# Phase 2 of a hybrid layer: transposes and their copy issued one tile ahead of the matmuls that use them

## Chip, cores and metric

The kernel runs on 8 cores of one Trainium2 chip. Every core runs the same program on its own data: a pair of cores shares one batch row of 8192 tokens, each producing half of it, and nothing is exchanged between cores. The metric is the device time of the slowest core in microseconds.

## What is computed

The reference is a layer of four residual steps on x of shape (4, 8192, 1024), cut here to what matters:

```python
# step 1: state-space like mixing (phases 1 and 2)
xn = layernorm(x)
proj = xn @ W_proj.T
delta, Bs, Cs, residual = split(proj, 4)
delta = softplus(delta @ W_delta.T + b_delta)
y = exp(delta * A1) * B1 * sum(xn * Cs) + cumsum(delta * B1) * sum(Cs)
x = x + y + residual * D
# step 2: feed-forward with a low-rank part folded into the weight (phase 2)
x = x + layernorm(x) @ (W + lora).T + b
# step 3: full self-attention of layernorm(x) (phase 3), then step 2 again
x = x + softmax(q @ k.T / 32) @ v
x = x + layernorm(x) @ (W + lora).T + b
```

## The kernel before

The program is written by hand: a small class collects each engine's instructions in the order in which the Python code adds them (`sch.add`), with waits on counting semaphores in front. So the order of the code is the order on every engine. VectorE, ScalarE and GpSimd also wait for their own previous instruction each time. TensorE has only the waits that are named; a wait whose count was already waited for on that engine is dropped.

Phase 1 (to about 1250 us) runs three 1024x1024 projections over 64 tiles of 128 tokens and writes delta and the residual part to DRAM. Phase 2 (about 1340 to 3500 us) is the subject. It loops over the same 64 tiles. Phase 3 computes attention in four passes over the keys, and in the last pass the second feed-forward.

Phase 2 for tile i consists of these parts:

- `p2loads(i)`: SyncE loads x, delta, the residual part and two carry rows.
- `p2A(i)`: step 1. GpSimd makes `g0b` (line 644) and D (661), TensorE a cumulative sum by a triangular matrix (650) and the carry (655), ScalarE the exponential E (664), VectorE G (666), GpSimd F (670) and D (673), VectorE E (675), and GpSimd the new x in F (679). F is p2F in the profile, and so on.
- `p2Bln(i)`: layer norm of F into `xn2b`, by the helper `ln`, whose lines 191 to 212 stand for all norms: a VectorE sum (191), small steps that alternate between ScalarE and VectorE, and the wide ScalarE step into bf16 (212).
- `p2B(i)`: step 2. Eight TensorE transposes (line 186, helper `transposes8`) into the PSUM tile PT1 or PT2, a ScalarE copy to `xn2T` (line 700), 16 matmuls into PB with `W_eff` (line 707), VectorE adds the bias into G (714), GpSimd adds F into H (717).
- `p2C(i)`: layer norm of H into `xn3b`, stored by ScalarE's queue; for the first 32 tiles H is stored too.

The loop body for i is: `p2C(i)`, `p2loads(i+3)`, `p2A(i+3)`, `p2Bln(i+2)`, `p2B(i+1)`. Buffers xn2b, xn2T, PT and H alternate between two, F and G rotate over three, PB is single.

Of the kernel before, what the change touches and what calls it, by code (L numbers as in the profile page):

```python
# [76 lines left out]
def build(phases=3, dbg=False, cut=None):  # L77
# [55 lines left out]
    TM = lambda m: ("t", m)  # L133
    VM = lambda m: ("v", m)
    SM = lambda m: ("s", m)
# [45 lines left out]
    def transposes8(pt, src_bf, waits=()):  # L181
        m = None
        for c in range(8):
            m = sch.add("tensor",
                        lambda e, o=pt[:, c, :], i_=src_bf[:, c * 128:(c + 1) * 128]:
                        e.transpose(o, i_, s_id[:, :]),
                        waits if c == 0 else (), inc=("t", 1) if c == 7 else None)
        return m
# [68 lines left out]
    try:  # L257
# [48 lines left out]
        for mch in range(8):  # L306
            p = mch % 2
# [297 lines left out]
        if phases >= 2:  # L605
# [11 lines left out]
            xn2b = [C2(nc.sbuf_tensor(f"xn2b{p}", [128, 1024], BF16)) for p in range(2)]  # L617
# [9 lines left out]
            mk2 = {}  # L627
# [58 lines left out]
            def p2Bln(i):  # L686
                p = i % 2
                q3 = i % 3
                mxn2 = ln(F_[q3], xn2b[p], st2[p], (GM(mk2[("x1", i)]),
                                                   TM(mk2.get(("tp2", i - 2), 0))))  # L690
                mk2[("xn2", i)] = mxn2

            def p2B(i):
                p = i % 2
                q3 = i % 3
                PTx = PT1 if p == 0 else PT2
                mxn2 = mk2[("xn2", i)]
                mtp2 = transposes8(PTx, xn2b[p], (SM(mxn2), SM(mk2.get(("ev2", i - 2), 0))))
                mk2[("tp2", i)] = mtp2
                mev2 = sch.add("scalar", lambda e, pp=p, pt=PTx: e.copy(  # L700
                    xn2T[pp][:, :, :], pt[:, :, :]),
                               (TM(mtp2),), inc=("s", 1))
                mk2[("ev2", i)] = mev2
                mf1 = None
                for n in range(2):
                    for k in range(8):
                        mf1 = sch.add("tensor", lambda e, nn=n, kk=k, pp=p: e.matmul(  # L707
                            PB[:, nn * 512:(nn + 1) * 512], xn2T[pp][:, kk, :],
                            W_eff[:, kk * 1024 + nn * 512: kk * 1024 + nn * 512 + 512],
                            start=(kk == 0), stop=(kk == 7)),  # L710
                            (SM(mev2), VM(mk2.get(("x2a", i - 1), 0)), VM(m_weff_v))
                            if (n == 0 and k == 0) else (),
                            inc=("t", 1) if (n == 1 and k == 7) else None)
                mx2a = sch.add("vector", lambda e, qq=q3: e.tensor_add(  # L714
                    G_[qq][:, :], PB[:, :], s_bfbc[:, :]), (TM(mf1),), inc=("v", 1))
                mk2[("x2a", i)] = mx2a
                mx2 = sch.add("gpsimd", lambda e, pp=p, qq=q3: e.tensor_add(  # L717
                    H_[pp][:, :], G_[qq][:, :], F_[qq][:, :]),
                    (VM(mx2a), mk2.get(("sx2", i - 2))), inc=("g", 1))
                mk2[("x2", i)] = mx2  # L720

            def p2C(i):
                p = i % 2
                mxn3 = ln(H_[p], xn3b[p], st3[p], (GM(mk2[("x2", i)]),
                                                   mk2.get(("sxn3", i - 2))))
                mk2[("sxn3", i)] = dma("scalar", sc_xn3[i, :, :], xn3b[p][:, :], ch=f"sx3{p}")
                if i < NQ:
                    mk2[("sx2", i)] = dma("scalar", sc_x2[i, :, :], H_[p][:, :],
                                          (GM(mk2[("x2", i)]),), ch=f"sx2{p}")

            def p2loads(i):
                p = i % 2
                mk2[("lx", i)] = dma("sync", A_[p][:, :], x_d[i * 128:(i + 1) * 128, :],
                                     (GM(mk2[("x1", i - 2)]),), ch=f"lA{p}")
                mk2[("lhi", i)] = dma("sync", hilo[p][0:1, :], sc_hi[i:i + 1, :],
                                      (TM(mk2[("tri", i - 2)]),), ch=f"lh{p}")
                mk2[("llo", i)] = dma("sync", hilo[p][1:2, :], sc_lo[i:i + 1, :], ch=f"lh{p}")
                mk2[("ldl", i)] = dma("vector", B_[p][:, :], sc_delta[i, :, :],
                                      (GM(mk2[("eIn", i - 2)]), mk[("dst", i)]), ch=f"lB{p}")
                mk2[("lr", i)] = dma("vector", Cc_[p][:, :], sc_res[i, :, :],  # L740
                                     (VM(mk2[("x1a", i - 2)]), mk[("rst", i)]), ch=f"lC{p}")
# [4 lines left out]
            p2A(2)  # L746
            p2Bln(0)
            p2Bln(1)
            p2B(0)
            for i in range(NT):  # L750
                p2C(i)
                if i + 3 < NT:
                    p2loads(i + 3)
                    p2A(i + 3)
                if i + 2 < NT:
                    p2Bln(i + 2)
                if i + 1 < NT:
                    p2B(i + 1)

# [464 lines left out]
```

How the kernel before makes its waits and increments, by code:

```python
        def f(eng):  # L1124
            for item in sch.prog[name]:
                if item[0] == "w":
                    eng.wait_ge(sems[item[1]], item[2])
                else:
                    _, fn, inc = item
                    ins = fn(eng)
                    if inc is not None:
                        ins.then_inc(sems[inc[0]], inc[1])
```

## Time and profile before

| what | us |
|---|---|
| median of 3 runs (lowest, highest) | 7283.0 (7268.4, 7551.5) |
| profiled execution, its own time | 7269.7 |
| span of its slowest core | 7268.1 |
| spans of the eight cores | 7255.8 to 7268.1 |
| TensorE busy (share of span) | 4472.4 (62%) |
| ScalarE busy | 2500.3 (34%) |
| VectorE busy | 1720.8 (24%) |
| GpSimd busy | 1323.9 (18%) |

The profile is one execution on the slowest core. Busy time is summed over the whole program, of which phase 2 is about 2150 us; what an engine does there must be read from that stretch. The granted clock is a share of 2.4 GHz: 0.50 is 1.2 GHz, 1.00 is 2.4 GHz. In the chain, "issue" is time in which the engine waited for nothing that the profile shows.

### The profile page before, as it was taken

How to read it: one execution, taken by the hardware profiler on the slowest of the kernel's cores; microseconds unless marked ns; L12 is line 12 of the kernel's file. 1: busy time of each engine (PE TensorE's matmuls, PEld its weight loads, DVE VectorE, ACT ScalarE, POOL GpSimd, SP SyncE). 2: the span in 40 equal slices, each digit the busy share in tenths (PEclk: the TensorE clock that was granted, in tenths of full speed). 3: DMA queues.
4: the chain of work that ended last, by engine and by line, in shares of the span. 5: the costliest groups of instructions: out<-in, count | busy, mean ns of one | idle time of the engine just before them, and what ended most of it. 6: DMA issues, size and time to landing. Idle time of an engine off the chain costs nothing.

```text
span 7268.1 us, 65317 instructions; the slowest of 8 cores (7255.8 to 7268.1 us)
## 1 busy us (share of the span) xinstructions
PE 4472.4 (62%) x20288; PEld 1967.8 (27%) x20288; DVE 1720.8 (24%) x2744; ACT 2500.3 (34%) x4418; POOL 1323.9 (18%) x611
## 2 busy tenths in 40 slices
PE   3889997122222222222578997999899865555555
PEld 1333333000000000000234443444344322222222
DVE  0223332122222222222002221332233122222221
ACT  0555553133333333333323332333233223222222
POOL 2222222434444434444000000000000000000000
PEclk8888887555555555555789999999999987777777
DMA  4222221421121111111220111222122101111110
GB/s 131 93 99 102 96 97 69 127 74 65 70 73 67 64 60 52 60 52 42 62 56 32 53 56 35 79 88 72 45 88 94 53 35 41 41 41 41 42 46 25
DMA packets 183210, 475.80 MB, mean 65 GB/s; under 512 B 51149, under 2 KB 51278, under 8 KB 182868
## 3 DMA queue, kind: packets, MB, share of 16 engines
q1 hardware_dynamic: 98740, 295.19, 12.8%
q10 hardware_dynamic: 84128, 176.45, 6.2%
q8 instruction: 167, 2.74, 0.2%
q14 instruction: 175, 1.43, 0.1%
HBM read 295.12 MB, written 176.42 MB: 65 GB/s over the span
## 4 chain that ended last, share of the span: by engine, by line
PE 50%; ACT 18%; DVE 12%; POOL 10%; issue 5%; DMA 3%; ACTq 1%; DVEq 0%; POOLq 0%; SPq 0%
PE PC L1017 13%; PE PA L924 6%; PE PB L924 6%; PE PB L707 5%; PE PA L864 4%; PE PB L883 3%; DVE st L191 3%; PE PC L1066 3%; PE PA L420 2%; POOL p2F L670 2%; POOL p2D L673 2%; POOL p2H L717 2%; ACT L208 2%; PE PA L814 2%; DVE st L210 2%
## 5 line engine op out<-in xcount | busy, mean ns | idle before, releaser
L1017 PE MATMUL PC<-v_res,pt_sb 128*128 128x512 bf16 x4096 | 994.8, 405 | 285.5 <-ACT pt_sb L1004 280.2
L707 PE MATMUL PB<-W_eff,xn2T 128*128 128x512 bf16 x1024 | 386.5, 560 | 1128.9 <-ACT xn2T L700 1128.9
L1078 POOL TENSOR_TENSOR s_out<-zs,x3b 128x1024 f32<-128x1024 f32 x32 | 75.0, 2343 | 3696.4 <-DVE zs L1073 3696.4
L1017 PEld LDWEIGHTS PC<-v_res,pt_sb 128*128 128x128 bf16 x4096 | 415.3, 103 | 814.0 <-issue 412.5
L707 PEld LDWEIGHTS PB<-W_eff,xn2T 128*128 128x128 bf16 x1024 | 132.3, 134 | 1368.3 <-issue 1350.9
L924 PE MATMUL PA<-kT_res,qT_t 128*128 128x512 bf16 x2048 | 471.4, 384 | 28.4 <-ACT P_bf L961 22.4
L924 PE MATMUL PB<-kT_res,qT_t 128*128 128x512 bf16 x2048 | 462.9, 379 | 0.0
L717 POOL TENSOR_TENSOR p2H<-p2G,p2F 128x1024 f32<-128x1024 f32 x64 | 149.6, 2337 | 828.1 <-DVE p2G L714 828.1
L193 ACT ACTIVATE s_sqscr<-p2H 128x1024 bf16<-128x1024 f32 x64 | 67.6, 1057 | 659.2 <-POOL p2H L717 659.2
L451 POOL TENSOR_TENSOR g_bf<-delta_f,s_B1bc 128x1024 bf16<-128x1024 f32 x64 | 150.3, 2348 | 782.7 <-ACT delta_f L442 782.7
L420 PE MATMUL PA<-W_dd,xnT 128*128 128x512 bf16 x1024 | 278.9, 435 | 3.5 <-DVE xnT L409 3.5
L924 PEld LDWEIGHTS PA<-kT_res,qT_t 128*128 128x128 bf16 x2048 | 201.7, 99 | 278.0 <-issue 43.9
L883 PE MATMUL PB<-WvT,xg3T 128*128 128x512 bf16 x1024 | 231.3, 379 | 70.9 <-DVE v_res L893 70.9
L893 DVE TENSOR_TENSOR v_res<-PB,s_bvbc 128x1024 bf16<-128x1024 f32 x64 | 78.4, 1225 | 814.7 <-PE PB L883 814.7
L864 PE MATMUL PA<-xg3T,WkT 128*128 128x512 bf16 x1024 | 255.2, 416 | 24.5 <-ACT xg3T L797 24.5
L924 PEld LDWEIGHTS PB<-kT_res,qT_t 128*128 128x128 bf16 x2048 | 200.4, 98 | 241.6
L462 PE MATMUL PA<-WrT,xnT 128*128 128x512 bf16 x1024 | 265.1, 419 | 0.0
L434 PE MATMUL PB<-WcT,xnT 128*128 128x512 bf16 x1024 | 264.7, 418 | 0.0
L934 DVE TENSOR_REDUCE cmax<-PB 128x1 f32<-128x512 f32 x256 | 177.1, 692 | 263.7 <-PE PB L924 263.7
L1031 DVE SCALAR_TENSOR_TENSOR zs<-zl,pstat,PC 128x1024 f32<-128x1024 f32 x96 | 122.9, 1280 | 488.0 <-PE PC L1017 488.0
L947 ACT ACTIVATE pstat<-pstat 128x1 f32<-128x1 f32 x96 | 19.5, 203 | 592.6 <-DVE pstat L945 592.3
L934 DVE TENSOR_REDUCE cmax<-PA 128x1 f32<-128x512 f32 x256 | 177.1, 692 | 189.0 <-PE PA L924 187.6
(164 smaller groups left out, 6640.1 us busy)
## 6 DMA issues: line engine op xcount, KB each, us to landing
sc_z<-zs ACTq DMA_DIRECT2D x96, 512.0 KB, 4.7
zl<-sc_z SPq DMA_DIRECT2D x96, 512.0 KB, 5.0
xb<-x SPq DMA_DIRECT2D x64, 512.0 KB, 3.4
sc_delta<-delta_f ACTq DMA_DIRECT2D x64, 512.0 KB, 2.7
sc_res<-res_f ACTq DMA_DIRECT2D x64, 512.0 KB, 2.7
p2A<-x SPq DMA_DIRECT2D x64, 512.0 KB, 5.2
p2B<-sc_delta SPq DMA_DIRECT2D x64, 512.0 KB, 5.3
p2C<-sc_res SPq DMA_DIRECT2D x64, 512.0 KB, 6.2
```

Source lines behind the costliest of these rows:

```text
L191: mv = sch.add("vector", lambda e: e.reduce_sum(stats[:, 0:1], xin[:, :], AX), w_x, inc=("v", 1))
L420: mdp = sch.add("tensor", lambda e, nn=n, kk=k, qq=q3: e.matmul(PA[:, nn * 512:(nn + 1) * 512], xnT[qq][:, kk, :], W_dd[:, kk * 1024 + nn ...
L434: mcs = sch.add("tensor", lambda e, nn=n, kk=k, qq=q3: e.matmul(PB[:, nn * 512:(nn + 1) * 512], xnT[qq][:, kk, :], WcT[:, kk * 1024 + nn * ...
L462: mrs = sch.add("tensor", lambda e, nn=n, kk=k, qq=q3: e.matmul(PA[:, nn * 512:(nn + 1) * 512], xnT[qq][:, kk, :], WrT[:, kk * 1024 + nn * ...
L707: mf1 = sch.add("tensor", lambda e, nn=n, kk=k, pp=p: e.matmul(PB[:, nn * 512:(nn + 1) * 512], xn2T[pp][:, kk, :], W_eff[:, kk * 1024 + nn ...
L717: mx2 = sch.add("gpsimd", lambda e, pp=p, qq=q3: e.tensor_add(H_[pp][:, :], G_[qq][:, :], F_[qq][:, :]), (VM(mx2a), mk2.get(("sx2", i - 2) ...
L864: mq = sch.add("tensor", lambda e, cc=c, kk=k, hh=half, pp=pg: e.matmul(PA[:, hh * 512:(hh + 1) * 512], WkT[:, kk * 1024 + cc * 128: kk * ...
L883: mv = sch.add("tensor", lambda e, nn=n, kk=k, tt=t, pp=pg: e.matmul(PB[:, nn * 512:(nn + 1) * 512], xg3T[pp][:, kk, tt * 128:(tt + 1) * 128],
L924: e.matmul(o[:, of:of + 512], qT_t[pp][:, cc, :], kT_res[:, cc, nn * 512:(nn + 1) * 512], start=(cc == 0), stop=(cc == 7)),
L934: mrx = sch.add("vector", lambda e, nn=n, o=ps_, of=off: e.reduce_max(cmax[:, nn:nn + 1], o[:, of:of + 512], AX), (TM(msmm),), inc=("v", 1))
L1017: mpv = sch.add("tensor", lambda e, jj=j, nn=n, pp=p: e.matmul(PC[:, nn * 512:(nn + 1) * 512], pt_sb[pp][:, jj, :], v_res[:, jj * 1024 + n ...
L1066: mf2 = sch.add("tensor", lambda e, nn=n, kk=k, pp=p: e.matmul(PC[:, nn * 512:(nn + 1) * 512], xn4T[pp].tensor[:, kk, :], W_eff[:, kk * 10 ...
```

## The change

`p2B` is split. Its transposes and the copy of line 700 become a function `p2Btp`, which the loop calls for tile i+2 right behind that tile's layer norm, ahead of the matmuls of tile i+1. The transposes get one more wait, on the matmuls of two tiles back (`f1`), since the copy behind them writes the buffer those matmuls read. Behind the change the matmul line is 712.

```diff
-            def p2B(i):
+            def p2Btp(i):
                 p = i % 2
-                q3 = i % 3
                 PTx = PT1 if p == 0 else PT2
                 mxn2 = mk2[("xn2", i)]
-                mtp2 = transposes8(PTx, xn2b[p], (SM(mxn2), SM(mk2.get(("ev2", i - 2), 0))))
+                mtp2 = transposes8(PTx, xn2b[p], (SM(mxn2), SM(mk2.get(("ev2", i - 2), 0)),
+                                                  TM(mk2.get(("f1", i - 2), 0))))
                 mk2[("tp2", i)] = mtp2
                 mev2 = sch.add("scalar", lambda e, pp=p, pt=PTx: e.copy(
                     xn2T[pp][:, :, :], pt[:, :, :]),
                                (TM(mtp2),), inc=("s", 1))
                 mk2[("ev2", i)] = mev2
+
+            def p2B(i):
+                p = i % 2
+                q3 = i % 3
+                mev2 = mk2[("ev2", i)]
                 mf1 = None
...
+                mk2[("f1", i)] = mf1
...
             p2Bln(0)
             p2Bln(1)
+            p2Btp(0)
+            p2Btp(1)
             p2B(0)
             for i in range(NT):
                 p2C(i)
...
                 if i + 2 < NT:
                     p2Bln(i + 2)
+                    p2Btp(i + 2)
                 if i + 1 < NT:
                     p2B(i + 1)
```

TensorE in the middle of the loop, before. The number at the end of a name is the buffer; PT1 and xn2b0 belong to even tiles, PT2 and xn2b1 to odd ones.

```order
L655 MATMUL PA<-hilo0,s_o2r 128x512 x2
L186 MATMUL PT1<-s_id,xn2b0 128x128 x8
L707 MATMUL PB<-W_eff,xn2T0 128x512 x16
L650 MATMUL PC<-p2g01,s_tri128 128x512 x2
L655 MATMUL PC<-hilo1,s_o2r 128x512 x2
L186 MATMUL PT2<-s_id,xn2b1 128x128 x8
L707 MATMUL PB<-W_eff,xn2T1 128x512 x16
```

The transposes stand in front of the matmuls of their own tile. The same place in the changed kernel:

```order
L655 MATMUL PA<-hilo0,s_o2r 128x512 x2
L186 MATMUL PT2<-s_id,xn2b1 128x128 x8
L712 MATMUL PB<-W_eff,xn2T0 128x512 x16
L650 MATMUL PC<-p2g01,s_tri128 128x512 x2
L655 MATMUL PC<-hilo1,s_o2r 128x512 x2
L186 MATMUL PT1<-s_id,xn2b0 128x128 x8
L712 MATMUL PB<-W_eff,xn2T1 128x512 x16
```

Now the transposes of the next tile stand in front of each group of matmuls. ScalarE at the end of one second norm and at the start of a third norm, before:

```order
L208 ACTIVATE st2_1<-st2_1 128x1
L212 ACTIVATE xn2b1<-p2F2,st2_1 128x1024
L700 COPY xn2T0<-PT1 128x1024
L193 ACTIVATE s_sqscr,st3_0<-p2H0 128x1024
L196 ACTIVATE st3_0<-st3_0 128x1
```

The copy behind the norm of an odd tile serves the even tile before it. And in the changed kernel:

```order
L208 ACTIVATE st2_1<-st2_1 128x1
L212 ACTIVATE xn2b1<-p2F2,st2_1 128x1024
L700 COPY xn2T1<-PT2 128x1024
L193 ACTIVATE s_sqscr,st3_0<-p2H0 128x1024
L196 ACTIVATE st3_0<-st3_0 128x1
```

The copy now belongs to the tile whose norm stands right before it.

## Rows read from the trace of the kernel before

**Rows 1.** The page's first line.

```profile
span 7268.1 us, 65317 instructions; the slowest of 8 cores (7255.8 to 7268.1 us)
```

**Rows 2.** Costliest groups, 1395 to 3500 us: count, busy us, mean ns, idle before.

```profile
L707 PE MATMUL PB<-W_eff,xn2T 128*128 128x512 bf16 x1024 | 386.5, 560 | 1128.9 <-ACT xn2T L700 1128.9
...
L700 ACT COPY xn2T<-PT 128x1024 bf16<-128x1024 bf16 x64 | 64.8, 1012 | 9.7 <-ACT xn3b L212 0.5 <-ACT xn2b L212 0.4
```

**Rows 3.** Chain that ended last, one round: start us, length us, what.

```profile
2519.66 4.93 PE PB L707 x16
...
2524.69 1.24 DVE p2G L714
...
2537.88 2.35 POOL p2F L670
...
2549.22 1.25 ACT xn2b L212
2550.60 1.02 ACT xn2T L700
...
2551.86 0.58 PE PB L707
```

**Rows 4.** Timeline of TensorE, bursts of line 707: start us, length us, [idle before].

```profile
1428.56 6.03 PE L707 MATMUL PB<-W_eff,xn2T 128*128 128x512 bf16 x16 [18.09 <-ACT xn2T L700]
...
2451.88 6.37 PE L707 MATMUL PB<-W_eff,xn2T 128*128 128x512 bf16 x16 [18.20 <-ACT xn2T L700]
...
2618.72 6.57 PE L707 MATMUL PB<-W_eff,xn2T 128*128 128x512 bf16 x16 [17.72 <-ACT xn2T L700]
...
2751.82 4.89 PE L707 MATMUL PB<-W_eff,xn2T 128*128 128x512 bf16 x16 [17.72 <-ACT xn2T L700]
...
3445.99 5.96 PE L707 MATMUL PB<-W_eff,xn2T 128*128 128x512 bf16 x16 [17.72 <-ACT xn2T L700]
```

**Rows 5.** Stretches inside two bursts: us, busy per engine, PEclk, DMA share, GB/s.

```profile
2451.88:2457.49 5.61, 5.61 (x14) 2.04 (x15) 0.50 0.25 100
2457.49:2458.25 0.76, 0.76 (x4) 0.14 (x2) 1.00 0.00 0
...
2752.00:2754.45 2.45, 2.45 (x7) 0.85 (x6) 0.00 (x0) 0.00 (x0) 0.00 (x0) 0.50 0.73 294
2754.45:2756.70 2.25, 2.25 (x11) 0.82 (x9) 0.00 (x0) 0.00 (x0) 0.00 (x0) 1.00 0.00 0
```

**Rows 6.** Timeline at the head of phase 2: first norm's end, first transposes.

```profile
1387.77 1.24 ACT L212 ACTIVATE xn2b<-p2F,st 128x1024 bf16<-128x1024 f32 x1 [0.36 <-DVE st L210]
...
1389.15 1.01 PE L186 MATMUL PT<-s_id,xn2b 128*128 128x128 bf16 x8 [14.27 <-ACT xn2b L212]
```

**Rows 7.** Timeline of TensorE in phase 1, around 275 us.

```profile
273.74 1.01 PE L481 MATMUL PC<-m_bf,s_emsk 128*128 128x512 bf16 x2 [1.73 <-POOL m_bf L455]
...
275.40 1.06 PE L186 MATMUL PT<-s_id,xn_bf 128*128 128x128 bf16 x8
276.25 3.68 PE L420 MATMUL PA<-W_dd,xnT 128*128 128x512 bf16 x16
```

**Rows 8.** Stretches at the same place of phase 1, columns as in rows 5.

```profile
273.74:276.37 2.63, 2.63 (x13) 1.53 (x14) 1.33 (x2) 1.90 (x6) 0.00 (x0) 0.50 0.00 0
276.37:279.77 3.40, 3.40 (x18) 1.50 (x17) 1.01 (x3) 2.70 (x3) 0.00 (x0) 1.00 0.00 0
```

**Rows 9.** Timeline of the last two tiles of phase 2.

```profile
3473.13 1.23 DVE L714 TENSOR_TENSOR p2G<-PB,s_bfbc 128x1024 f32<-128x1024 f32 x1 [8.22 <-PE PB L707]
...
3480.34 0.16 DVE L210 TENSOR_TENSOR st<-st 128x1 f32<-128x1 f32 x1 [0.40 <-ACT st L208]
...
3483.60 5.93 PE L707 MATMUL PB<-W_eff,xn2T 128*128 128x512 bf16 x16 [10.12 <-ACT xn2T L700]
3489.63 1.22 DVE L714 TENSOR_TENSOR p2G<-PB,s_bfbc 128x1024 f32<-128x1024 f32 x1 [9.14 <-PE PB L707]
```

**Rows 10.** Timeline of ScalarE behind one copy: start of the third norm.

```profile
2528.61 1.06 ACT L193 ACTIVATE s_sqscr<-p2H 128x1024 bf16<-128x1024 f32 x1 [9.20 <-POOL p2H L717]
```

## The prediction

> **What bounds the kernel now.** The chain of waits puts nothing of the change outside the tile loop of phase 2, so I read in this order: the costliest groups (how much lines 700 and 707 cost), the timeline of one loop round, the chain through that round, and then the granted clock inside single bursts. The profiled execution took 7269.7 us, its span is 7268.1 us [rows 1]; the median of the runs shown is 7283.0 us, so the same gain counts from either.
>
> Line 707 is 64 bursts of 16 matmuls, busy 386.5 us, so 6.04 us a burst, and TensorE sat idle 1128.9 us before them waiting for the ScalarE copy of line 700, which costs 1.01 us each [rows 2]. One round as the chain shows it [rows 3]: the burst of tile 33 starts at 2519.66 and takes 4.93; VectorE adds the bias at 2524.69, then come GpSimd's sum into H, the third layer norm, the exponential and GpSimd's p2F at 2537.88, the second layer norm up to xn2b at 2549.22 (1.25), the copy into xn2T at 2550.60 (1.02), and the next burst at 2551.86. No engine is busy half of that round; it is one ring of dependent steps of different tiles, tied together by the program order of ScalarE and VectorE. What leaves the ring shortens the round by its full length. From the end of xn2b (2549.22 + 1.24 = 2550.46) to the first matmul there are 1.40 us.
>
> The burst itself is the second variable. Bursts last from 4.89 to 6.57 us [rows 4], and the cause is the clock: in the burst at 2451.88 TensorE had 0.50 (1.2 GHz) for 5.61 us and 1.00 (2.4 GHz) for the last 0.76; in the one at 2751.82 it had 0.50 up to 2754.45, that is 2.63 us, and 1.00 behind [rows 5]. The two give the price: 2.98 us less at the low level made the burst 6.37 - 4.89 = 1.48 us shorter, 0.50 us per us. The longest, 6.57 us, thus rose 2.63 + 1.68 / 0.497 = 6.0 us in. So the rise comes 2.6 to 6.0 us behind the first matmul. In the first half it sits near the late end: between bursts 1 and 31 [rows 4] lie 30 rounds of (2451.88 - 1428.56) / 30 = 34.11 us, with bursts of 6.0 to 6.4 us.
>
> **The change part by part.** It moves the eight transposes and the copy of line 700 one tile ahead. ScalarE's order then is xn2b(i+2), copy(i+2) instead of xn2b(i+2), copy(i+1); TensorE's is transposes(i+2), matmuls(i+1) instead of transposes(i+1), matmuls(i+1). So the copy that matmuls(i+1) need was made a round earlier, but these matmuls now stand in TensorE's queue behind transposes that wait for xn2b(i+2).
>
> Term 1, the hand-over. Removed from the ring: 1.40 us. Added: ScalarE's end to TensorE's start, then eight transposes. For the start the nearest row with two semaphores to pass is copy to burst, 2550.60 + 1.01 to 2551.86, 0.25 us [rows 3]; with one, xn2b to transposes at the head of phase 2, 1387.77 + 1.24 to 1389.15, 0.14 [rows 6]. The changed transposes pass two (xn2b, and the new one on the old burst), so I take 0.25. The eight transposes cost 0.85 us before a matmul that follows directly (275.40 to 276.25 [rows 7]) and at most their whole 1.01 us [rows 6]. New hand-over 0.25 + 0.85 = 1.10, gain 0.30 us; bounds 1.40 - 0.25 - 1.01 = 0.14 and 1.40 - 0.14 - 0.85 = 0.41. It applies to the bursts of tiles 1 to 62: 62 x 0.30 = 18.6 us (9 to 25).
>
> Term 2, the clock. TensorE now works 0.85 us without a gap before the first matmul, where it had been idle for 18 us [rows 4]. Do transposes bring the rise nearer? In phase 1 they did: TensorE idled 1.73 us to 273.74, ran four matmuls and the eight transposes to 276.25, had 0.50 up to 276.37 and 1.00 from there [rows 7, 8]. That is 2.63 us of work in a row, 0.85 of it transposes, and the same 2.63 us as the earliest rise in a burst of matmuls alone. So I count transposes like matmuls: the rise, from the first matmul, comes 0.85 us sooner at both ends, 1.8 to 5.2 us. The Trainium skill speaks against it: "TensorE: Matmul & The Clock Gate", Part 4, PE-mode transpose, says that the full clock doesn't engage for transposes because they don't count as busy in the same way. By that rule term 2 would be nothing; the phase 1 rows disagree with it.
>
> Where in 1.8 to 5.2 will the bursts lie? The even beat of the first half can't stay: a round without its burst is 34.13 - 6.37 = 27.76 us there, 27.46 after term 1, and with the longest burst now possible (rise at 5.2: 4.89 + 2.57 x 0.497 = 6.17) the round is 33.6, below 34.1. So bursts should wander over the whole range, as they do today in the second half (6.57 at 2618.72, 4.89 at 2751.82), where 28 rounds last (3445.99 - 2519.66) / 28 = 33.08 us [rows 3, 4]. Even spread: rise at 3.5, burst 4.89 + 0.87 x 0.497 = 5.32 us against 6.04: 0.72 x 62 = 44.6 us. Bounds: 0 if the rise keeps its distance from the matmuls, and 6.04 - 4.48 = 1.56 us (97 us) if each burst met the earliest rise.
>
> Term 3, the end of phase 2. The last burst has no newer tile before it. Today it starts at 3483.60, behind the third norm of tile 62 and its copy, and VectorE takes its sum at 3489.63 [rows 9]. Its copy will be long done, so it can start when VectorE has emptied PB (3473.13 + 1.23, plus 0.25 = 3474.6) and end by 3478.2 at the high clock (3.6 us by the price above) or 3481.7 at the low one (7.1). VectorE's order puts its sum behind the small step at 3480.34 + 0.16: at 3480.5 or 3481.8, 7.8 to 9.1 us sooner. I take 9.
>
> At nothing: the copy of line 700 itself. It now waits on ScalarE for transposes that end about 1.3 us behind xn2b, ends 2.5 us behind it, and the next ScalarE step is idle for 9.20 us before 2528.61 [rows 10]. Without that cover it would delay the third norm, 1.3 us a round. The added wait on the burst two tiles back is long met; only its passing is paid, in term 1. DMA issues, GpSimd and SyncE keep their order. The head gains nothing: the first burst waits for the second xn2b as before, then its copy.
>
> Sum: 18.6 + 44.6 + 9 = 72 us. From 7269.7 that is 7198; from the median 7283 it is 7211. I say 7205.
>
> **The rivals.** (a) Transposes don't move the clock. Then only terms 1 and 3: 28 us, at most, 7242 to 7255; and in the first half a matmul that starts 0.30 sooner just waits 0.30 longer for the rise, which can hold the 34.1 beat and leave 18 us. For it: 2.63 us was met in one phase 1 stretch only, mixed with matmuls. Against it: that stretch had just 1.8 us of matmuls. (b) Slower: with the transposes first, the rise is put off past the end of the burst, the queue runs cold to the end. A burst that sees no rise is, by the price of 0.50 per us, 7.1 us (4.89 + 4.47 x 0.497), 1.07 more than the mean now; less 0.30, times 62, less 8: 40 us slower, 7310 to 7323. It decides from the point where a rise comes over 7 us behind the first matmul, on line 707 in every tile. Against it: more work ahead has not delayed a rise in any row. (c) The beat locks at an early rise: with burst 4.5 to 4.9 us each, 1.14 to 1.56 us per tile, 71 to 97 us plus 28: 99 to 125 us faster, 7158 to 7184. Against it: a short burst brings the next start forward, away from the rise (behind the 4.93 at 2519.66 the round is 32.20 instead of 34.1 [rows 3]), so the next one is longer.
>
> **How the numbers follow.** Forecast 0.74 (own range 7180 to 7235), (a) 0.17, (b) 0.04, (c) 0.05. The range 7178 to 7262 takes in (a) and leaves out (b) and most of (c). A change of 2% is about what a measurement of this kernel can tell: 145 us faster would need more than (c), 0.02; slower needs over three times (b), 0.01; within 2%, 0.97.
>
> **What would show it.** Right: the copy's start no longer precedes the burst; transposes and burst adjoin, 1.1 us from xn2b to the first matmul; busy time of the burst group near 340 us instead of 386.5; rounds of the first half under 33.3 us; the last burst starts 9 us after its predecessor's end at the latest; phase 3 unchanged. Wrong in term 1: 1.4 us or more between xn2b and matmul. Wrong in term 2: burst group still near 386 us, rise never below 2.6 us behind the first matmul. The forecast as a whole is wrong if phase 3, which does not change, moves by more than a few us, or if the third norm starts later behind its GpSimd sum than today.

## The result: 0.9% faster, all of it in phase 2

| | before | changed |
|---|---|---|
| median of 26 runs, us | 7393.9 | 7333.5 |
| lowest run, us | 7268.4 | 7207.4 |
| profiled execution, us | 7269.7 | 7240.0 |
| ratio, 95% interval | 1 | 0.9914 (0.9881 to 0.9947) |

In at least half of the 26 runs of either kernel some cores had a lower TensorE clock, whichever the kernel, and these runs lie up to 6% above the lowest, so both medians are higher than the 7283 of three runs that stood at the start, and the ratio comes from the other runs. The lowest runs lie 60.9 us apart, the ratio says 39 to 87 us of 7283. The forecast was 72 us.

The profile of the changed kernel, its first line, then the groups of its transposes and of its bursts (columns as in rows 2):

```profile
span 7238.5 us, 65380 instructions; the slowest of 8 cores (7172.3 to 7238.5 us)
L186 PE MATMUL PT<-s_id,xn2b 128*128 128x128 bf16 x512 | 64.7, 306 | 1120.0 <-ACT xn2b L212 1120.0
L712 PE MATMUL PB<-W_eff,xn2T 128*128 128x512 bf16 x1024 | 346.9, 513 | 1.6 <-DVE p2G L720 1.5
```

The bursts are busy 346.9 us instead of 386.5 [rows 2], 5.42 us each. The 1.1 ms in which TensorE waits now stand in front of the transposes and are released by xn2b; the matmuls wait for nothing. One round in the timeline, which answers to rows 3:

```profile
2446.43 1.24 ACT L212 ACTIVATE xn2b<-p2F,st 128x1024 bf16<-128x1024 f32 x1 [0.36 <-DVE st L210]
2447.93 1.01 PE L186 MATMUL PT<-s_id,xn2b 128*128 128x128 bf16 x8 [18.02 <-ACT xn2b L212]
2448.74 6.17 PE L712 MATMUL PB<-W_eff,xn2T 128*128 128x512 bf16 x16
2449.03 1.01 ACT L700 COPY xn2T<-PT 128x1024 bf16<-128x1024 bf16 x1 [1.36 <-PE PT L186]
2455.02 1.23 DVE L720 TENSOR_TENSOR p2G<-PB,s_bfbc 128x1024 f32<-128x1024 f32 x1 [8.68 <-PE PB L712]
...
2458.93 1.06 ACT L193 ACTIVATE s_sqscr<-p2H 128x1024 bf16<-128x1024 f32 x1 [8.89 <-POOL p2H L723]
```

From the end of xn2b (2447.67) to the first matmul there are 1.07 us where there were 1.40. The copy starts behind the first matmul, is over at 2450.04, and ScalarE then still idles 8.89 us. That is the hand-over as forecast. The clock, in the shortest kind of burst, by the timeline and then by stretches (busy, PEclk, DMA share, GB/s), which answer to rows 4 and 5:

```profile
2284.01 1.01 PE L186 MATMUL PT<-s_id,xn2b 128*128 128x128 bf16 x8 [18.01 <-ACT xn2b L212]
2284.82 4.53 PE L712 MATMUL PB<-W_eff,xn2T 128*128 128x512 bf16 x16
```

```profile
2284.82:2286.65 1.83, 1.83 (x7) 0.50 0.80 287
2286.65:2289.35 2.70, 2.69 (x13) 1.00 0.05 21
```

The rise to 2.4 GHz comes 1.83 us behind the first matmul; before, none came sooner than 2.62. The burst at 2448.74 above is at the other end: 6.17 us, with the rise about 5.2 us in. The end of phase 2, which answers to rows 9:

```profile
3409.95 5.15 PE L712 MATMUL PB<-W_eff,xn2T 128*128 128x512 bf16 x16
3416.58 3.61 PE L712 MATMUL PB<-W_eff,xn2T 128*128 128x512 bf16 x16 [1.48 <-DVE p2G L720]
```

```profile
3415.21 1.22 DVE L720 TENSOR_TENSOR p2G<-PB,s_bfbc 128x1024 f32<-128x1024 f32 x1 [7.65 <-PE PB L712]
...
3422.42 0.16 DVE L210 TENSOR_TENSOR st<-st 128x1 f32<-128x1 f32 x1 [0.40 <-ACT st L208]
3422.75 1.22 DVE L720 TENSOR_TENSOR p2G<-PB,s_bfbc 128x1024 f32<-128x1024 f32 x1 [0.17 <-DVE st L210]
```

The last burst waits only for VectorE to empty PB; the last bias add starts 3422.75 - 3415.21 = 7.5 us behind that of tile 62, where it was 3489.63 - 3473.13 = 16.5 [rows 9], 9.0 less.

To compare kernels I use the time from the start of the first burst to the start of the last on cores 0 and 3. It does not depend on phase 3. Before: 2088.0 and 2088.4 us; changed: 2021.1 and 2020.6. So phase 2 gave 67 us. The slowest core of the changed profile shows only 30 of them; these are the stretches from some 10 us behind the last burst to the end, so phase 3, first core 3 before, then core 3 and core 5 of the changed kernel (length, busy PE, PEld, DVE, ACT, POOL, then PEclk, DMA share, GB/s):

```profile
3500.00:7268.00 3768.00, 2884.91 (x14336) 1343.66 (x14336) 836.41 (x1568) 1185.21 (x2303) 74.97 (x32) 0.87 0.16 54
```

```profile
3430.00:7199.00 3769.00, 2886.70 (x14336) 1344.24 (x14336) 836.39 (x1568) 1185.91 (x2303) 74.98 (x32) 0.87 0.16 54
...
3430.00:7238.00 3808.00, 2924.16 (x14336) 1355.62 (x14336) 835.63 (x1569) 1188.18 (x2303) 74.98 (x32) 0.85 0.16 54
```

On core 3 phase 3 is unchanged (3768 and 3769 us). Core 5 had a granted clock of 0.85 instead of 0.87 there and took 39 us more for the same matmuls; since core 3 of the same execution shows nothing of it, I don't count it to the change.

### The profile page after: what moved, and what is told of

It is laid out like the page before. It is cut to its first block, busy times and chain, and to the rows that moved or that the text cites. A ratio compares the mean times of both kernels' runs of the same rounds, so it can differ in the third digit from the quotient of the medians.

```text
span 7238.5 us, 65380 instructions; the slowest of 8 cores (7172.3 to 7238.5 us)
## 1 busy us (share of the span) xinstructions
PE 4414.9 (61%) x20288; PEld 1966.2 (27%) x20288; DVE 1719.5 (24%) x2744; ACT 2503.5 (35%) x4418; POOL 1323.7 (18%) x611
## 4 chain that ended last, share of the span: by engine, by line
PE 50%; ACT 17%; DVE 12%; POOL 11%; issue 5%; DMA 3%; ACTq 1%; DVEq 0%; POOLq 0%; SPq 0%
PE PC L1026 13%; PE PA L933 6%; PE PB L933 6%; PE PB L712 5%; PE PA L873 3%; PE PB L892 3%; DVE st L191 3%; PE PA L420 3%; PE PC L1075 3%; PE PT L186 2%; POOL p2F L670 2%; POOL p2D L673 2%; POOL p2H L723 2%; ACT L208 2%; POOL g_bf L451 2%
## 5 line engine op out<-in xcount | busy, mean ns | idle before, releaser
L186 PE MATMUL PT<-s_id,xn2b 128*128 128x128 bf16 x512 | 64.7, 306 | 1120.0 <-ACT xn2b L212 1120.0
L933 PE MATMUL PA<-kT_res,qT_t 128*128 128x512 bf16 x2048 | 486.8, 393 | 28.4 <-ACT P_bf L970 22.5
L933 PE MATMUL PB<-kT_res,qT_t 128*128 128x512 bf16 x2048 | 478.1, 388 | 0.0
L186 PEld LDWEIGHTS PT<-s_id,xn2b 128*128 128x128 bf16 x512 | 49.5, 137 | 1175.1 <-issue 1175.1
L712 PE MATMUL PB<-W_eff,xn2T 128*128 128x512 bf16 x1024 | 346.9, 513 | 1.6 <-DVE p2G L720 1.5
L434 PE MATMUL PB<-WcT,xnT 128*128 128x512 bf16 x1024 | 239.0, 388 | 0.0
L462 PE MATMUL PA<-WrT,xnT 128*128 128x512 bf16 x1024 | 239.0, 388 | 0.0
```

The lines of the kernel that those rows point to most:

```text
L434: mcs = sch.add("tensor", lambda e, nn=n, kk=k, qq=q3: e.matmul(PB[:, nn * 512:(nn + 1) * 512], xnT[qq][:, kk, :], WcT[:, kk * 1024 + nn * ...
L462: mrs = sch.add("tensor", lambda e, nn=n, kk=k, qq=q3: e.matmul(PA[:, nn * 512:(nn + 1) * 512], xnT[qq][:, kk, :], WrT[:, kk * 1024 + nn * ...
L933: e.matmul(o[:, of:of + 512], qT_t[pp][:, cc, :], kT_res[:, cc, nn * 512:(nn + 1) * 512], start=(cc == 0), stop=(cc == 7)),
```

## Experiments

My theory was the sum of the forecast: a hand-over (the time from the end of xn2b to the first matmul) shortened by 0.3 us a round (term 1), transposes that bring the clock's rise nearer to the matmuls (term 2), and a last burst that no longer waits (term 3). The rivals were that the transposes don't move the clock, that the end hides the last burst, and, for the ring itself, that another engine becomes the bound once something leaves it.

All eight, with the time from the first to the last burst of phase 2 on cores 0 and 3:

| kernel | first to last burst, us | mean burst, us (core 0) | ratio to before (95%) |
|---|---|---|---|
| before | 2088.0, 2088.4 | 6.03 | 1 |
| changed | 2021.1, 2020.6 | 5.42 | 0.9914 (0.9881 to 0.9947) |
| e1 last tile alone | 2080.3, 2078.8 | 6.01 | 1.0027 (0.9973 to 1.0081) |
| e2 transposes alone | 2044.8, 2045.4 | 5.35 | none |
| e3 more transposes beside the ring | 1992.8, 1994.5 | 4.98 | 0.9884 (0.9836 to 0.9933) |
| e5 more transposes on the ring | 2037.1, 2036.3 | 4.96 | 0.9915 (0.9885 to 0.9944) |
| e4 burst before the norm | 1481.7, 1481.9 | 5.60 | 0.9151 (0.9115 to 0.9187) |
| e6 sum of F first | 1446.8, 1447.2 | 5.75 | 0.9141 (0.9097 to 0.9185) |
| e7 sum into H held back | 1423.9, 1425.4 | 5.72 | 0.9060 (0.8947 to 0.9173) |
| e8 small steps on ScalarE | 1336.8, 1338.2 | 5.66 | 0.8906 (0.8797 to 0.9015) |

### e1: the last tile alone

The main part of the edit, against the changed kernel:

```diff
                 if i + 2 < NT:
                     p2Bln(i + 2)
-                    p2Btp(i + 2)
                 if i + 1 < NT:
+                    if i + 1 < NT - 1:
+                        p2Btp(i + 1)
                     p2B(i + 1)
+                    if i + 1 == NT - 2:
+                        p2Btp(NT - 1)
```

> Order of before, but the transposes and the copy of tile 63 alone are issued behind the matmuls of tile 62, so the last burst waits for nothing but PB. Theory (term 3): the last burst starts right behind the bias add of tile 62 and the program ends 8 to 9 us sooner than before, about 0.12%, all of it behind 3467 us; rounds before that keep 34.1 and 33.1 us. Rival (the gain of the change came from the rounds alone and the end of phase 2 hides the last burst anyway): 0 us.

The timeline of core 1, last two tiles:

```profile
3486.12 1.23 DVE L720 TENSOR_TENSOR p2G<-PB,s_bfbc 128x1024 f32<-128x1024 f32 x1 [8.22 <-PE PB L712]
...
3487.82 3.61 PE L712 MATMUL PB<-W_eff,xn2T 128*128 128x512 bf16 x16 [1.36 <-ACT xn2T L700]
...
3493.67 1.22 DVE L720 TENSOR_TENSOR p2G<-PB,s_bfbc 128x1024 f32<-128x1024 f32 x1 [0.17 <-DVE st L210]
```

From the bias add of tile 62 to the last: 3493.67 - 3486.12 = 7.55 us against 16.50 [rows 9], 8.95 less. Rounds kept 34.1 us in the first half and 33.1 in the second, and first to last burst fell by 7.7 and 9.6. Term 3 is 9 us, as forecast. The ratio's interval is plus or minus 39 us, so whole-program time can't show an effect of this size; the trace does.

### e2: transposes ahead, copy where it was

Against the changed kernel:

```diff
                 if i + 2 < NT:
                     p2Bln(i + 2)
                     p2Btp(i + 2)
                 if i + 1 < NT:
+                    p2Bcp(i + 1)
                     p2B(i + 1)
```

Here `p2Btp` has the transposes alone and `p2Bcp` the copy of line 700.

> Only the transposes move one tile ahead; the copy stays where it was, between xn2b(i+2) and the matmuls of tile i+1. The hand-over from xn2b to the first matmul stays 1.40 us and nothing leaves the ring, so terms 1 and 3 are out and term 2 is alone. Theory (transposes count for the clock as matmuls do): rise 1.8 to 5.2 us behind the first matmul, bursts about 5.3 to 5.5 us instead of 6.04, phase 2 shorter by 35 to 45 us. Rival (transposes do not move the clock): bursts stay near 6.04 us, rise never below 2.6 us, 0 us gained.

One hand-over on core 2, in the timeline:

```profile
2437.09 1.24 ACT L212 ACTIVATE xn2b<-p2F,st 128x1024 bf16<-128x1024 f32 x1 [0.36 <-DVE st L210]
2438.47 1.01 ACT L705 COPY xn2T<-PT 128x1024 bf16<-128x1024 bf16 x1
...
2438.58 1.01 PE L186 MATMUL PT<-s_id,xn2b 128*128 128x128 bf16 x8 [18.01 <-ACT xn2b L212]
...
2439.74 5.46 PE L717 MATMUL PB<-W_eff,xn2T 128*128 128x512 bf16 x16
```

The hand-over is 2438.33 to 2439.74, 1.41 us: nothing left the ring. Still bursts fell from 6.03 to 5.35 us and rounds from 34.1 to 33.3 and from 33.1 to 32.5; first to last burst is 43 us shorter. That is term 2 by itself, forecast at 44.6. The stretches of one of the shortest bursts, on core 3 (busy PE, PEclk, DMA share, GB/s):

```profile
1504.43:1506.21 1.78, 1.78 (x5) 0.50 0.55 196
1506.21:1508.90 2.69, 2.69 (x13) 1.00 0.03 14
```

The rival is out: its 0 us and its 6.04 us bursts didn't come, and the rise lies 1.8 to 5.2 us behind the first matmul on that core, as expected. The whole program gave no ratio: in the profiled execution, the lowest of six, the cores took 7206.8 to 7251.9 us, where before they took 7255.8 to 7268.1. The verdict rests on the trace of phase 2.

### e3: eight more transposes that nothing waits for

Against the changed kernel, without the lines that pass `mv4` on:

```diff
+                for c in range(8):
+                    sch.add("tensor", lambda e, o=PTx[:, c, :]: e.transpose(
+                        o, s_id[:, :], s_id[:, :]),
+                        (VM(mk2[("mv4", i)]), SM(mk2.get(("ev2", i - 2), 0)))
+                        if c == 0 else ())
                 mtp2 = transposes8(PTx, xn2b[p], (SM(mxn2), SM(mk2.get(("ev2", i - 2), 0)),
```

`mv4` is the last small step of the norm. The extra transposes are overwritten by the real ones.

> The changed kernel plus eight more transposes of the identity per tile, released by the last small norm step, so that they run while ScalarE writes xn2b and are overwritten by the real ones; nothing in the ring waits for them. Theory: another 0.85 us of work ahead of each burst brings the rise to about 0.9 to 4.3 us behind the first matmul; the mean burst falls from 5.42 to about 5.0 us, 62 x 0.42 = 26 us more than the changed kernel, some 90 to 95 us below before. Rival (what counts is only work without a gap): no more than the changed kernel, burst 5.42 us. Second rival (the extra transposes delay the real ones): slower than the changed kernel by up to 60 x 0.4 us.

Timeline of core 0, then the stretches of a short burst on it:

```profile
2423.92 1.24 ACT L214 ACTIVATE xn2b<-p2F,st 128x1024 bf16<-128x1024 f32 x1 [0.36 <-DVE st L212]
2423.97 1.01 PE L702 MATMUL PT<-s_id 128*128 128x128 bf16 x8 [16.58 <-DVE st L212]
2425.41 1.01 PE L186 MATMUL PT<-s_id,xn2b 128*128 128x128 bf16 x8 [0.43 <-ACT xn2b L214]
2426.22 5.53 PE L721 MATMUL PB<-W_eff,xn2T 128*128 128x512 bf16 x16
```

```profile
2490.29:2491.52 1.23, 1.23 (x5) 0.50 0.69 240
2491.52:2494.50 2.98, 2.98 (x14) 1.00 0.16 63
```

The extra work runs beside xn2b, 0.43 us of idle time apart from the real transposes, and the hand-over keeps 1.06 us. Bursts fall to 4.98 us, first to last burst by another 26 to 28 us against the changed kernel (26 expected). The rise to 1.00 lay 1.0 to 4.35 us behind the first matmul, against 0.9 to 4.3 expected; in 11 of the 64 bursts on core 0 the clock rose to 0.81 only, so the gain is, if anything, larger than measured. So the idle gap of 0.43 us does no harm, and both rivals are out. Work of no use, placed where TensorE waits, makes phase 2 of this kernel faster. By whole-program time the intervals of e3 and of the changed kernel overlap; their lowest runs are 7173.4 and 7207.4 us.

### e5: the same transposes on the ring

Against e3:

```diff
-                        (VM(mk2[("mv4", i)]), SM(mk2.get(("ev2", i - 2), 0)))
+                        (SM(mxn2), SM(mk2.get(("ev2", i - 2), 0)))
                         if c == 0 else ())
```

> The changed kernel with the hand-over doubled: eight transposes of the identity, released by xn2b, run ahead of the eight real ones, so that 0.85 us more lie on the ring and 0.85 us more work lies ahead of each burst. Theory (both terms hold and add): round + 0.85 us for the hand-over, burst 0.42 us shorter for an earlier rise, as e3 showed with the same transposes off the ring; net + 0.43 x 62 = 27 us against the changed kernel, about 45 us below before; from xn2b to the first matmul 1.9 us. Rival (the hand-over is hidden by something else and only the clock counts): 26 us faster than the changed kernel, as e3.

```profile
2109.22 1.24 ACT L212 ACTIVATE xn2b<-p2F,st 128x1024 bf16<-128x1024 f32 x1 [0.36 <-DVE st L210]
2110.61 1.01 PE L698 MATMUL PT<-s_id 128*128 128x128 bf16 x8 [17.91 <-ACT xn2b L212]
...
2111.41 1.06 PE L186 MATMUL PT<-s_id,xn2b 128*128 128x128 bf16 x8
...
2112.26 5.35 PE L716 MATMUL PB<-W_eff,xn2T 128*128 128x512 bf16 x16
```

The timeline of core 5 has 1.80 us from xn2b's end (2110.46) to the first matmul, 0.73 more than the changed kernel. Bursts are as short as in e3 (4.96, rise 1.0 to 4.4 us behind the first matmul), and first to last burst is 16 us longer than in the changed kernel and 42 to 44 us longer than in e3. Between e3 and e5 only the place of the transposes differs: 43 us for 62 x 0.73 = 45 us more on the ring. The hand-over counts in full, as term 1 says. The net against the changed kernel was 16 us, not 27, since 0.73 and not 0.85 us were added and the bursts gained 0.46.

### e4: the burst before the second norm

```diff
-                if i + 2 < NT:
-                    p2Bln(i + 2)
                 if i + 1 < NT:
                     p2B(i + 1)
+                if i + 2 < NT:
+                    p2Bln(i + 2)
```

This is the kernel before with two calls exchanged.

> Order of before with two calls exchanged: transposes, copy and matmuls of tile i+1 come ahead of the second norm of tile i+2, in the stretch where ScalarE waits 6.65 us for the VectorE sum. Theory (phase 2 is one ring of steps, and what leaves it shortens the round by its length): burst, bias add, sum into H and hand-over run beside GpSimd's F and D; the ring keeps the third norm, exponential, F, D, E and second norm, with about 2.3 us more before the second norm's sum because VectorE takes the bias add first: 24.2 us a round instead of 33.6, 9.4 x 60 = about 560 us faster. Rival (GpSimd, 14 us of work a round, or the loads become the bound as soon as the burst is out): rounds of 28 us or more, less than 350 us.

Timeline of core 7 in the first half:

```profile
2101.19 1.01 ACT L700 COPY xn2T<-PT 128x1024 bf16<-128x1024 bf16 x1
...
2102.50 6.11 PE L707 MATMUL PB<-W_eff,xn2T 128*128 128x512 bf16 x16 [8.05 <-ACT xn2T L700]
...
2106.26 1.28 DVE L675 SCALAR_TENSOR_TENSOR p2E<-p2C,s_Dbc,p2D 128x1024 f32<-128x1024 f32 x1 [8.47 <-POOL p2D L673]
...
2108.71 1.22 DVE L714 TENSOR_TENSOR p2G<-PB,s_bfbc 128x1024 f32<-128x1024 f32 x1 [1.17 <-PE PB L707]
...
2116.79 1.06 ACT L193 ACTIVATE s_sqscr<-p2H 128x1024 bf16<-128x1024 f32 x1 [0.20 <-ACT xn2b L212]
```

The burst runs while GpSimd makes F and D, and the third norm of the next tile follows the second norm at once (idle 0.20 us, where before ScalarE sat 9.20 us [rows 10]). Rounds: 24.0 and 23.4 us, first to last burst 606 us shorter, the program 6670.9 us. The ring picture gave 24.2 us a round; the rival (28 us or more) is out. The change studied here took 0.33 us of hand-over and 0.6 us of burst off the ring; the exchange, with the same instructions, takes off the hand-over, the sum and the burst but for its last 1.17 us, for which VectorE waits; the bias add stays (1.22 us).

### e6: VectorE's sum of F ahead of the bias add

The main part of the edit, against the kernel before:

```diff
+        if hook is not None:
+            hook()
         msq = sch.add("scalar", lambda e: e.activation(s_sqscr[:, :], xin[:, :], AF.Square,
...
+                if i + 1 < NT:
+                    p2B(i + 1)
                 if i + 2 < NT:
-                    p2Bln(i + 2)
-                if i + 1 < NT:
-                    p2B(i + 1)
+                    p2Bln(i + 2, lambda ii=i + 1: p2Bx(ii))
+                elif i + 1 < NT:
+                    p2Bx(i + 1)
```

`p2Bx` is the bias add and the sum into H; the hook stands behind the first VectorE step of the norm.

> As e4, but VectorE takes the sum of F (first step of the second norm) ahead of the bias add of tile i+1, which then lies in the 2.2 us in which VectorE waits for ScalarE's small steps. Theory: in e4's round VectorE's wait for the burst (1.17 us) and the bias add (1.33 us with its start) are on the ring; both leave it, 2.4 us x 60 = 145 us less than e4, rounds of 21.5 us, about 6525 us. Rival (GpSimd's sum into H comes late and delays the third norm): rounds stay near 23.9 us, no gain on e4.

A miss in half: rounds of 22.8 us up to tile 32, but 23.5 behind it, where e4 had 23.4. Timeline of core 5 behind tile 32:

```profile
2605.89 1.22 DVE L722 TENSOR_TENSOR p2G<-PB,s_bfbc 128x1024 f32<-128x1024 f32 x1 [0.17 <-DVE st L191]
...
2607.26 2.34 POOL L725 TENSOR_TENSOR p2H<-p2G,p2F 128x1024 f32<-128x1024 f32 x1 [0.37 <-DVE p2G L722]
2607.29 2.33 DVE L204 TENSOR_TENSOR st<-st 128x1 f32<-128x1 f32 x1 [0.17 <-DVE p2G L722]
```

A step on 128 single numbers took 2.33 us and ended with GpSimd's sum, behind which it had started by 0.03 us. The gain of the new order was eaten by that: behind tile 32 the small two-operand steps take 2.3 us a round more than their 0.16 each, up to there 1.1. The rival I had named (the sum into H comes late) is not what happened.

### e7: GpSimd's sum held back

```diff
-                    (VM(mx2a), mk2.get(("sx2", i - 2))), inc=("g", 1))
+                    (VM(mx2a), VM(mlater), mk2.get(("sx2", i - 2))), inc=("g", 1))
```

This is against e6. `mlater` is the small difference of the second norm; to have it, the sum is added behind that norm, which leaves the order on every engine as it was.

> As e6, but GpSimd's sum into H (2.34 us) also waits for the small VectorE difference in the second norm. In e6, behind tile 32, that difference started 0.03 us behind GpSimd's sum and took 2.33 us instead of 0.16, ending with it. Theory (a small VectorE step with two operands that starts while GpSimd runs a wide one ends only with it): the difference takes 0.16 us again, rounds behind tile 32 fall from 23.5 to about 21.4 us, 2.1 x 30 = 60 us less than e6; in the first half, where the difference was already ahead, 22.7 us stays. Rival (the difference waits for something else, such as the bias add's write): it still takes about 2.3 us and rounds stay at 23.5 us.

Core 5, same place of the loop, in both norms:

```profile
2599.02 0.16 DVE L206 TENSOR_TENSOR st<-st 128x1 f32<-128x1 f32 x1 [0.17 <-DVE p2G L725]
...
2599.32 2.34 POOL L733 TENSOR_TENSOR p2H<-p2G,p2F 128x1024 f32<-128x1024 f32 x1 [0.70 <-DVE st L206]
2599.57 0.16 DVE L211 RECIPROCAL st<-st 128x1 f32<-128x1 f32 x1 [0.40 <-ACT st L209]
...
2604.41 2.34 POOL L666 TENSOR_TENSOR p2D<-p2B,s_A1bc 128x1024 f32<-128x1024 f32 x1
2605.40 1.37 DVE L206 TENSOR_TENSOR st<-st 128x1 f32<-128x1 f32 x1 [2.27 <-ACT st L204]
```

The difference takes 0.16 us once it starts ahead of GpSimd, which tells the two theories apart. The rounds behind tile 32 fell from 23.5 to 22.5 us and not to 21.4, because the delayed GpSimd work now meets the same step of the third norm: 1.37 us at 2605.40, ending at 2606.77 with GpSimd's product (2604.41 + 2.34 = 2606.75). Over a round the hold-ups fell by 1.0 us behind tile 32, as the rounds did. Up to tile 32 they grew by 0.3 us, and the rounds rose from 22.8 to 23.1, where I had expected no change; so phase 2 is only 23 us shorter than in e6, not 60. The reciprocal, with one operand, ran in 0.16 us in the middle of a GpSimd sum. The Trainium skill has this rule: by "SBUF — State Buffer", section "SBUF: two separate sides", a VectorE step with two inputs in SBUF and a GpSimd step that reads SBUF share a port pair, and the one that starts first locks it for its whole instruction. The trace agrees, with 2.33 and 1.37 us for a step of 0.16.

### e8: the small steps on ScalarE

```diff
-        mv2 = sch.add("vector", lambda e: e.tensor_sub(stats[:, 5:6], stats[:, 3:4],
-                                                       stats[:, 4:5]), (SM(ms), SM(mvh)), inc=("v", 1))
+        mv2 = sch.add("scalar", lambda e: e.activation(stats[:, 5:6], stats[:, 4:5], AF.Identity,
+                                                       bias=stats[:, 3:4], scale=-1.0),
+                      (SM(ms), SM(mvh)), inc=("s", 1))
...
-        mv4 = sch.add("vector", lambda e: e.tensor_mul(stats[:, 9:10], stats[:, 2:3],
-                                                       stats[:, 8:9]), (SM(ms3),), inc=("v", 1))
+        mv4 = sch.add("scalar", lambda e: e.activation(stats[:, 9:10], stats[:, 2:3], AF.Identity,
+                                                       scale=stats[:, 8:9]), (SM(ms3),), inc=("s", 1))
```

It is built on e6, without e7's wait.

> As e6, but the two small VectorE steps with two operands of every layer norm (difference and product) run on ScalarE as activations with bias or scale from the stats tile; all phases. Theory: these steps cannot be held up by GpSimd any more, and four changes of engine per round (0.3 us each) go: rounds of about 20.5 us in both halves instead of 22.7 and 23.5, phase 2 shorter by 2.6 x 62 = 160 us than in e6, and the 32 norms of the last attention pass, which lie on its chain, give 32 x 0.6 = 20 us more: about 6470 us. Rival (GpSimd's 14 us of work and the reciprocal are held up instead, so the time moves to the next step): less than 60 us gained on e6.

Timeline of core 3 behind tile 32:

```profile
2598.67 0.29 ACT L204 ACTIVATE st<-st 128x1 f32<-128x1 f32 x1
2599.24 2.34 POOL L726 TENSOR_TENSOR p2H<-p2G,p2F 128x1024 f32<-128x1024 f32 x1 [0.37 <-DVE p2G L723]
2599.36 0.16 DVE L209 RECIPROCAL st<-st 128x1 f32<-128x1 f32 x1 [0.27 <-ACT st L207]
...
2601.19 0.29 ACT L213 ACTIVATE st<-st 128x1 f32<-128x1 f32 x1
2601.58 1.24 ACT L215 ACTIVATE xn2b<-p2F,st 128x1024 bf16<-128x1024 f32 x1
```

No small step is held up, and the ones moved to ScalarE take 0.29 us without a change of engine. Rounds are 21.6 and 21.1 us (20.5 expected), phase 2 is 110 us shorter than in e6 (160 expected), and the program's span is 6511.1 us against e6's 6645.4. The expected size was too large, its rival's 60 us too small. The traces say what the gain is made of. The hold-ups of e6, 1.1 us a round up to tile 32 and 2.3 behind it, are gone, and the rounds are 1.15 and 2.4 us shorter; so the changes of engine that I had priced at 0.3 us each, 1.2 a round, gave about 0.1. At 0.8906 (0.8797 to 0.9015) e8 is the fastest kernel here, and beats both the kernel before and the changed one.

I had overlooked that the kernel before has such a hold-up too. Its timeline, core 3, in the third norm:

```profile
2531.21 2.34 POOL L661 TENSOR_TENSOR p2D<-p2B,s_A1bc 128x1024 f32<-128x1024 f32 x1
...
2532.04 1.53 DVE L210 TENSOR_TENSOR st<-st 128x1 f32<-128x1 f32 x1 [0.40 <-ACT st L208]
```

The small product takes 1.53 us instead of 0.16 and ends at 2533.57, with GpSimd's step (2533.55); ScalarE waits for it before it can write xn3b. This stands in 58 of the 64 rounds of the kernel before and of the changed one. It lies on the ring, so by an estimate from these rows, 1.37 x 58, it costs up to 79 us, more than the change gave. No run took it away by itself.

## Where the prediction held and where it didn't

- Term 1, 18.6 us. The hand-over came out at 1.07 us against the forecast 1.10, so 0.33 x 62 = 20 us left the ring, and the price of a microsecond there is confirmed by e3 against e5. But only 15 of the 67 us are left after e2 (43) and the last tile (9): with the shorter hand-over the bursts are 0.07 us longer than in e2 (5.42 against 5.35), some 4 us. Right in mechanism; that the two terms add in full was not.
- Term 2, 44.6 us. Mean burst 5.42 (forecast 5.32), so 0.61 x 62 = 38 us in the changed kernel, and 43 us by itself in e2; range of the rise 1.8 to 5.2 us behind the first matmul, as forecast. The even beat of 34.1 us is gone: 32.9 us a round in the first half. Right, and by the mechanism named; it was 7 us too large and term 1, at 20, was 1 to 2 too small, which makes 67 of the 72. The sentence of the Trainium skill that spoke against it ("TensorE: Matmul & The Clock Gate", Part 4) doesn't hold here: transposes did bring the rise nearer, in e2, e3 and e5.
- Term 3, 9 us: 9.0 in the changed kernel, 8.95 in e1. Right.
- At nothing: ScalarE still idles 8.89 us behind the moved copy. Right. One sign of being wrong came up: phase 3 moved, by 39 us on core 5, but by 1 us on core 3, where the clock was the same.
- Rival (a) falls with e2, (b) and (c) with the bursts themselves: none ran at the low level to its end, and short ones alternate with long ones.
- Wrong, the absolute time: the last line of the sum, "From 7269.7 that is 7198; from the median 7283 it is 7211. I say 7205." The size of 72 us is inside the measured 39 to 87, and the lowest run is 7207.4; but the median of 26 runs is 7333.5, outside 7178 to 7262. I tied the absolute time to a median of three runs, of which the highest was already 268 us above it, and gave the range for the effect alone. With 26 runs of the kernel before, that anchor is 7393.9. The term that was mis-sized is the base, by 111 us, not the change. That the lowest run came within 3 us of 7205 is partly luck: counted from the lowest run before, 7268.4, the 72 us give 7196.

## To carry to other kernels

Before moving a copy or a transpose by one step, write down the ring of steps that sets a round, and ask which of its large members could run beside it: here issuing the transposes and the copy a tile ahead gave 67 us, while exchanging two calls gave 606. Look also for steps that take longer than their size explains: a small product in this ring took 1.53 us for 0.16. Where TensorE works in bursts between waits, look at when the clock rises within a burst; in this kernel work placed ahead of it, even useless work, is paid back at half a microsecond per microsecond as long as it lies beside the ring. And give an absolute time no narrower than the runs of the kernel before are spread.

## What the hardware showed that I had not expected

- A VectorE step on 128x1 with two operands took 2.33 us instead of 0.16 when it started 0.03 us behind a wide GpSimd step, and ended with it (e6); that is enough to undo a better order.
- Useless transposes 0.43 us of idle time apart from the real ones shortened the bursts as much (4.98 us, e3) as ones without a gap (4.96, e5).
- In the kernel before, most rounds of the first half repeated at 34.1 us to within 0.3, since a later start met the rise sooner and made its burst shorter. On core 3 a round of 34.45 us, 0.33 longer than the one before it, led to a burst at 1633.03 whose rise came 5.26 us behind its first matmul instead of 5.58 and which took 6.20 us instead of 6.35; the next round was 33.96. Such a loop can give back part of a small gain, as e2 against the changed kernel shows: by that rule alone the first half would have kept its beat, had the transposes not moved the rise as well. That last point is argued from the rows, not tried.
